# Two cross-attentions in one kernel: where the next context is split, and what the key transfers wait for

## The reference

```
x = x + tanh(g_xattn[0]) * attention_0(layernorm(x), context)     # 16 heads of 32
x = x + tanh(g_ffn[0])   * bit_linear_conv_ffn(layernorm(x))
x = x + tanh(g_xattn[1]) * attention_1(layernorm(x), context, mask)  # 8 heads of 64
x = x + tanh(g_ffn[1])   * fp4_ffn(layernorm(x))

attention: q = x Wq; k = context Wk; v = context Wv
           softmax(q k^T / sqrt(d)) v, heads joined, times Wo
```

## Time and profile before

| | before |
|---|---|
| median of 3 executions | 2663.02 us |
| profiled execution: time | 2659.33 us |
| profiled execution: span, mean granted clock of TensorE | 2657.5 us, 0.885 |
| PE (matmuls) busy | 2027.9 us, 76% |
| DVE busy | 1655.1 us, 62% |
| ACT busy | 952.9 us, 36% |
| POOL busy | 950.8 us, 36% |
| weight loads of PE (beside the matmuls) | 1410.6 us, 53% |

### The profile page before, as it was taken

How to read it: one execution, slowest core, us unless ns; L and a number is a source line. 1 busy time by engine, 2 the same in 40 slices (tenths; PEclk the granted TensorE clock), 3 DMA queues, 4 the chain that set the end, 5 groups by cost and what they waited for, 6 DMA issues and landing times. The chain is left out here.

```text
span 2657.5 us, 42241 instructions
## 1 busy us (share of the span) xinstructions
PE 2027.9 (76%) x15208; PEld 1410.6 (53%) x15208; DVE 1655.1 (62%) x3011; ACT 952.9 (36%) x1299; POOL 950.8 (36%) x518
## 2 busy tenths in 40 slices
PE   3688888788887078888489999998997125788887
PEld 2366566566565077777246666666665113344443
DVE  3656655665662887887444455545543998777773
ACT  2155555555566223333224443444434111111110
POOL 4054444444456321221302222222224563433442
PEclk8898998999896589999689999999998557888888
DMA  4232322333220301010433323333321200001000
GB/s 156 56 82 70 96 78 76 91 88 85 78 57 25 138 15 40 23 41 28 140 84 92 104 79 93 102 102 81 92 79 41 93 30 12 20 28 32 24 20 28
DMA packets 152278, 179.25 MB, mean 67 GB/s; under 512 B 60456, under 2 KB 120104, under 8 KB 151592
## 3 DMA queue, kind: packets, MB, share of 16 engines
q1 hardware_dynamic: 152104, 176.86, 23.1%
HBM read 129.96 MB, written 46.60 MB: 66 GB/s over the span
## 5 line engine op out<-in xcount | busy, mean ns | idle before, releaser
L545 POOL TENSOR_TENSOR a_p_hl<-a_p,a_p_hl 125x1344 bf16<-125x1344 f32 x192 | 525.0, 2735 | 953.9 <-ACT a_p_hl L643 953.3
L871 PE MATMUL a_psum<-a_chl,a_w 128*128 128x375 bf16 x1536 | 305.0, 356 | 55.4 <-DVE a_chl L718 45.6
L960 PE MATMUL a_psum<-a_k_st,a_q_st 96*112 96x375 bf16 (+2 forms) x1024 | 257.2, 344 | 111.3 <-DVE a_nm L778 68.9
L643 ACT ACTIVATE a_p_hl<-a_p 125x1344 bf16<-125x1344 f32 x192 | 254.0, 1323 | 121.7 <-PE a_psum L978 118.8
L633 ACT ACTIVATE a_p<-a_psum 125x1344 f32<-125x1344 f32 x192 | 247.8, 1291 | 132.5 <-PE a_psum L940 128.7
L871 PE MATMUL a_psum<-a_w,a_chl 128*125 128x512 bf16 x1152 | 269.8, 384 | 1.5 <-DVE a_xnT L748 0.9
L778 DVE TENSOR_REDUCE a_nm<-a_psum 112x1 f32<-112x750 f32 x256 | 236.1, 930 | 49.7 <-PE a_psum L960 47.4
L871 PEld LDWEIGHTS a_psum<-a_chl,a_w 128*128 128x128 bf16 x1536 | 158.0, 106 | 176.6 <-issue 88.3
L940 PE MATMUL a_psum<-a_q_st,a_k_st 99*125 99x224 bf16 (+2 forms) x1536 | 222.6, 268 | 5.2 <-ACT a_p L633 5.1
L960 PEld LDWEIGHTS a_psum<-a_k_st,a_q_st 96*112 96x112 bf16 (+2 forms) x1024 | 107.6, 131 | 196.3 <-DVE a_nm L778 89.6
L978 PEld LDWEIGHTS a_psum<-a_v_st,a_p_hl 125*128 125x128 bf16 x4608 | 180.4, 99 | 39.5 <-issue 22.9
(11 more groups left out here) (203 smaller groups left out, 3388.6 us busy)
## 6 DMA issues: line engine op xcount, KB each, us to landing
a_k_st<-a_k SPq DMA_DIRECT2D x192, 187.5 KB, 3.4
a_c<-in_ctx_t SPq DMA_DIRECT2D x32, 750.0 KB, 5.4
a_k<-a_k_tmp SPq DMA_DIRECT2D x64, 375.0 KB, 3.0
a_q_st<-a_q SPq DMA_DIRECT2D x192, 56.0 KB, 2.9
a_q<-a_q_tmp SPq DMA_DIRECT2D x64, 112.0 KB, 1.9
x<-a_xo SPq DMA_DIRECT2D x32, 224.0 KB, 2.3
f_w<-in_w1T SPq DMA_DIRECT2D x4, 1024.0 KB, 11.1
f_w<-in_w2T SPq DMA_DIRECT2D x4, 1024.0 KB, 16.7
```

Source lines behind the costliest of these rows:

```text
L545: nc.gpsimd.tensor_tensor(p_hl[0:MC, h % 2, 1, :], p32[0:MC, h % 2, :], p_hl[0:MC, h % 2, 0, :], ALU.subtract).then_inc(plo_done, 1)
L643: nc.scalar.activation(p_hl[0:MC, par, 0, :], p32[0:MC, par, :], ACT.Copy).then_inc(phi_done, 1)
L871: ins = nc.tensor.matmul(out, lhs, rhs, start=(c == 0 and n == 0), stop=(c == KC - 1 and n == 2))
L960: ins = nc.tensor.matmul(sm_[0:HALF, kh, 0:MK], q_stack(b.parity, at(h), rows)[:, s * HALF:(s + 1) * HALF], k_stack(b.parity, at(h), rows) ...
```

## The change

For items 2 to 7 the first half of the next context is now split in the third quarter, right behind unit K(3, 1) of the item before. SP orders the second half behind the query transfers of chunk 3, still in the third quarter. ACT writes its high part at the start of the fourth quarter, DVE its low part at the second head of the fourth quarter, before that head's units. For item 1, in the prologue, all stays as it was.

On SP one function, `regroup`, replaces two. It serves keys and queries in turn: store, wait for that store alone, then the three transfers into the stack. `kq_sent` becomes `k_sent` and `q_sent`, so an attention has one semaphore more. The semaphores of A0 stay taken until POOL clears and frees them at the start of the first FFN; those of A1 stay taken.

The diff, less the lines that only drop the counter `n_sent`; the condition `b.number == 1` replaces `b.number != 0` on ACT as it does on DVE:

```diff
--- before.py
+++ after.py
@@ -173,8 +173,12 @@
         def pb(name, shape):
             return ctx.enter_context(nc.psum_tensor(f"{tag}_{name}", shape, F32))

+        sems = []
+
         def sem(name):
-            return ctx.enter_context(nc.semaphore(f"{tag}_{name}"))
+
+            sems.append(nc.alloc_semaphore(f"{tag}_{name}"))
+            return sems[-1]


         q_dram = nc.dram_tensor(f"{tag}_q", (KC, 2, P, S), BF16, kind="Internal").ap()
@@ -240,7 +244,7 @@
         st_in = [sem(f"st_in{c}") for c in range(KC)]
         m_in = [sem(f"m_in{g}") for g in range(2)]
         out_sent = sem("out_sent")
-        kq_sent = sem("kq_sent")
+        k_sent, q_sent = sem("k_sent"), sem("q_sent")
         sp_steps = sem("sp_steps")
         preset = sem("preset")
         w_hi, w_lo, gate_ready = sem("w_hi"), sem("w_lo"), sem("gate_ready")
@@ -393,31 +396,22 @@
                 sp.dma_start(x_out[bass.ds(at, 1), s:s + 1, :, :].rearrange(
                     "o s p d -> p (o s d)"), xo[:, s, :]).then_inc(out_sent, 16)

-            def send_k(cc, n_done):
-
+            def regroup(b, cc, n_done, sent, tmp, dram, stack, width, parts):

                 sp.wait_ge(unit_done, n_done)
-                sp.dma_start(k_dram[cc].rearrange("a p m -> p a m"), k_tmp[:, cc % 2, :, :]).then_inc(kq_sent, 16)
-
-            def send_q_and_regroup(b, cc, n_done):
-
-                n_done, n_both = value(n_done), value(n_sent.next() * 32)
+                sp.dma_start(dram[cc].rearrange("a p n -> p a n"), tmp[:, cc % 2, :, :]).then_inc(sent, 16)
                 n_used = value((b.index - 1) * H + (cc + 1) * HC)
-                sp.wait_ge(unit_done, n_done)
-                sp.dma_start(q_dram[cc].rearrange("a p s -> p a s"), q_tmp[:, cc % 2, :, :]).then_inc(kq_sent, 16)
-
-                sp.wait_ge(kq_sent, n_both)
+                n_sent = value((b.index * KC + cc + 1) * 16)
                 if b.number is None or b.number >= 2:
                     settle()

                     sp.wait_ge(st_ready, n_used)
-                for stack, tmp, width, parts in ((k_st, k_dram, M, (0, 1, 0)), (q_st, q_dram, S, (0, 0, 1))):
-                    for (row, col), part in zip(((0, 0), (32, 0), (64, 0)) if stacked else ((0, 0), (64, 0), (0, 8)),
-                                                parts):
-                        c0 = col + cc * HC
-                        sp.dma_start(stack[row:row + DK, b.parity, c0 * width:(c0 + HC) * width].rearrange(
-                            "p (h n) -> p h n", h=HC), tmp[cc, part].rearrange(
-                            "(h p) n -> p h n", h=HC)).then_inc(st_in[cc], 16)
+                sp.wait_ge(sent, n_sent)
+                for (row, col), part in zip(((0, 0), (32, 0), (64, 0)) if stacked else ((0, 0), (64, 0), (0, 8)), parts):
+                    c0 = col + cc * HC
+                    sp.dma_start(stack[row:row + DK, b.parity, c0 * width:(c0 + HC) * width].rearrange(
+                        "p (h n) -> p h n", h=HC), dram[cc, part].rearrange(
+                        "(h p) n -> p h n", h=HC)).then_inc(st_in[cc], 16)

             def move_maxima(b, g, n_done):
                 sp.wait_ge(unit_done, n_done)
@@ -431,9 +425,9 @@
                 kind, k, b = unit
                 n = units.next()
                 if kind == "K" and k[1] == 1:
-                    send_k(k[0], value(n))
+                    regroup(b, k[0], value(n), k_sent, k_tmp, k_dram, k_st, M, (0, 1, 0))
                 elif kind == "Q":
-                    send_q_and_regroup(b, k, n)
+                    regroup(b, k, value(n), q_sent, q_tmp, q_dram, q_st, S, (0, 0, 1))
                 elif kind == "M":
                     move_maxima(b, k, n)
                 elif kind == "OP":
@@ -456,13 +450,12 @@
                     load_x(b + 2)
                     load_ctx(b + 2, 0)
                     load_masks(b + 2)
-                if q == 3:
-                    if (b + 2).exists():
-                        load_ctx(b + 2, 1)
                 if q == 0 and (b + -1).exists():
                     load_residual(b + -1)
                 for unit in quarter_units(q, b) + last_unit(q, b):
                     after_unit(unit)
+                    if unit[:2] == ("Q", KC - 1) and (b + 2).exists():
+                        load_ctx(b + 2, 1)


             sp.sem_inc(out_sent, 1)
@@ -659,22 +650,28 @@

             def quarter(q, b):
                 if q == 3 and (b + 2).exists():
-                    split_ctx(b + 2, 0, units.base + units.k)
+                    split_ctx(b + 2, 1, units.base + units.k)
                 if q == 1 and (b + 1).exists():
                     mask_bias_t(b + 1)
                 slots = slots_of(q, b)
+
+                def unit_step(unit):
+                    unit_hi_part(unit)
+                    if unit[:2] == ("K", (KC - 1, 1)) and (b + 2).exists():
+                        split_ctx(b + 2, 0, None)
+
                 for j in range(HC):
                     for unit in slots[4 * j]:
-                        unit_hi_part(unit)
+                        unit_step(unit)
                     if b.exists():
                         exponentials(b, q * HC + j)
                     for unit in slots[4 * j + 1]:
-                        unit_hi_part(unit)
+                        unit_step(unit)
                     if b.exists():
                         exponentials_hi(b, q * HC + j)
                     for k in (2, 3):
                         for unit in slots[4 * j + k]:
-                            unit_hi_part(unit)
+                            unit_step(unit)
                 if q == 3 and (b + 2).exists():
                     mask_bias(b + 2)
                 for unit in last_unit(q, b):
@@ -720,7 +717,7 @@

             def unit_lo_part(unit):
                 kind, k, b = unit
-                if unit[:2] == ("K", (0, 0)) and b.number != 0:
+                if unit[:2] == ("K", (0, 0)) and b.number == 1:
                     split_ctx(b, 1)
                 n = units.next()
                 bank = units.bank()
@@ -809,14 +806,20 @@
                     unit_lo_part(step)

             def quarter(q, b):
-                if q == 3 and (b + 2).exists():
-                    split_ctx(b + 2, 0)
                 slots = slots_of(q, b)
+
+                def unit_step(unit):
+                    unit_lo_part(unit)
+                    if unit[:2] == ("K", (KC - 1, 1)) and (b + 2).exists():
+                        split_ctx(b + 2, 0)
+
                 for j in range(HC):
                     h = q * HC + j
+                    if q == 3 and j == 1 and (b + 2).exists():
+                        split_ctx(b + 2, 1)
                     for k in (0, 1):
                         for unit in slots[4 * j + k]:
-                            unit_lo_part(unit)
+                            unit_step(unit)
                     preparing = q == 2 and (b + 2).exists()
                     if preparing and j == HC - 1:
                         normalise(b + 2)
@@ -1019,13 +1022,15 @@

             walk(pe.Fori, quarter, prologue, units.enter_loop, units.leave_loop)

+    return sems
+

 LINKS_PER_ROW = 44 - 14

 ROUND = 1.5 * 2.0 ** 23


-def bit_ffn(nc, tag, x_in, x_out, w1T, conv_w, conv_b, w2T, gate):
+def bit_ffn(nc, tag, x_in, x_out, w1T, conv_w, conv_b, w2T, gate, old_sems):

@@ -1185,6 +1190,7 @@

         @block.gpsimd
         def _(pool):
+            nc.clear_and_free_semaphores(old_sems)
             nc.gpsimd.memset(ones[:, :], 1.0).then_inc(preset, 1)
             pool.wait_ge(preset, 1)
             nc.gpsimd.memset(ident[:, :], 0.0).then_inc(preset, 1)
@@ -2018,8 +2024,8 @@
             Wq1, Wkv1, Wo1, w_gate, w_up, w_down, out):

     x1, x2, x3 = (nc.dram_tensor(f"x{n}", (B, 2, HALF, D), F32, kind="Internal").ap() for n in (1, 2, 3))
-    cross_attention(nc, "a0", x, x1, ctx_t, (Wq0T, Wk0T, Wv0T, Wo0T), g_xattn[0:1], None, 16)
-    bit_ffn(nc, "f0", x1, x2, w1T, conv_w, conv_b, w2T, g_ffn[0:1])
+    a0_sems = cross_attention(nc, "a0", x, x1, ctx_t, (Wq0T, Wk0T, Wv0T, Wo0T), g_xattn[0:1], None, 16)
+    bit_ffn(nc, "f0", x1, x2, w1T, conv_w, conv_b, w2T, g_ffn[0:1], a0_sems)
     cross_attention(nc, "a1", x2, x3, ctx_t, (Wq1, Wkv1[:, 0:D], Wkv1[:, D:2 * D], Wo1), g_xattn[1:2],
                     (mask, mask_t), 8)
     fp4_ffn(nc, "f1", x3, out, w_gate, w_up, w_down, g_ffn[1:2])
```

More of the change, by code:

```diff
@@ L334, in _ @@
             units = Units()
-            n_sent = Units(KC)
             def value(v):
@@ L479, in enter @@
                 units.enter_loop(i)
-                n_sent.enter_loop(i)
             def leave():
                 units.leave_loop()
-                n_sent.leave_loop()
             walk(sp.Fori, quarter, prologue, enter, leave)
```

## The result

The change made the kernel slower: 2688.88 us (median of 4 runs, 2685.82 to 2695.31) against 2664.22 us before (4 runs beside them), a ratio of 1.0095 with a 95% interval of 1.0074 to 1.0115. I had forecast 2646 us and a range of 2627 to 2665. The profiled execution took 2688.89 us (span 2687.1, granted clock 0.875 against 0.885), 29.6 us more than the one before.

The account below looks back on a forecast made before the run. PE was taken to set a row's pace, with its waits at the seam between rows to win. A0's rows -15.9, A1's -5.9 and prologues +5.2 made -16.6 us: about 2646 us, range 2627 to 2665.

Parts of the forecast that it names:

- A0's seam: First attention, fourth quarter: the stretch through the second key projection falls from 18.55 to 13.6 us, 4.9 us gained per seam.
- A0's third quarter: First attention: the moved first-half split makes PE wait, 2.0 us per row, plus 0.85 us for a possible clock drop.
- rival C: A0's third-quarter split runs 3.0 us because of POOL's subtraction and the clock falls: slower, 2675 us; chance 0.11.
- A0's transfers: First attention, seam: key stacks go earlier and query stacks at 615.4 instead of 616.1, 0.6 us gained per row.
- A1's seam load: Second attention: the second half's load, behind the third quarter's transfers, lands slightly late for ACT; +0.2 us per row net.
- Rival D: The second half's load takes 7.2 us, ACT stands at both attentions' seams, 21.6 us back: 2668 us; chance 0.17.
- A1's stack waits: Second attention, seams: query stacks go 2 us earlier, so PE's wait for them, 7.1 us over six seams, goes.
- The wait for the split in A1: Second attention, seam: PE's 2.84 us wait before the second key projection, and the slow projection behind it, stay.
- The prologues: Both attentions' prologues: query stores behind the keys' landing lengthen PE's and ACT's waits, 5.2 us together (0 to 8).
- Semaphores: Start of the first FFN: POOL clearing A0's 40 semaphores costs nothing, at most 2 us.

Follow-up runs that it names:

- e1: The kernel before with only the transfers changed (keys: store, wait, stacks; then queries), splits and context loads as before: ratio 0.9992 to the kernel before.
- e4: The changed kernel with the load of the next context's second half issued ahead of the third quarter's query unit, in both attentions: ratio 0.9954 to the kernel before.
- e7: Kernel of e6, with A1's second-half load ahead of the query unit and DVE's split ahead of K(0,0)'s low part: 2612.73 us, 0.9814 to the kernel before.
- e5: Kernel before with splits moved in A0 alone; in both attentions both stores issued first, then keys' and queries' stacks each behind their own store: 2623 us, ratio 0.9855.
- e10: The changed kernel with both stores issued before the keys' stacks for items 0 and 1 only: 2672.06 us, ratio 1.0024 to the kernel before.
- e9: The kernel before with only its transfers changed to the order of e5, splits and loads as before: 2641 us, ratio 0.9905.
- e6: The kernel of e5 with the splits moved in A1 too, the second-half load behind the third quarter's query unit: ratio 0.9834 to the kernel before.

## Why the prediction was wrong

By its own steps:

- **A0's seam (13.6 us, -4.9)**: right, 13.35 us and -5.2.
- **A0's third quarter (+2.0, clock +0.85)**: right. PE waits 2.15 us where it waited 0.35, and the query projection behind takes 1.93 us instead of 1.31, the clock's part. All six splits there take 1.73 us, so rival C did not happen.
- **A0's transfers (-0.6 a row)**: not borne out. The query stacks go 3.5 us behind their store (612.29 to 615.80), where the sum had 2.0 from the earlier trace rows, and the wait for the stacks did not fall: 19.6 us over A0's loop (19.2 in e1), before 18.8. That the row as a whole came out right (-2.7 for -2.65) owes something to luck: this term was too good and the third quarter's too bad (2.2 us from the product at 575.80 to the one at 592.95 against those at 573.97 and 588.96, where the sum had 2.85).
- **A1's seam load (+0.2 a row)**: the step that failed most. Its place and its path, ACT in order and from it PE, were named rightly, and the slack of ACT was 0.7 us (a wait of 4.66 us there reached PE as 3.96) where the sum had 0.8. But ACT waits 2.25 to 4.66 us, and the sum had 1.1. What failed is the chain of landings ahead of the load: the queries' store was priced at a landing of 2.0 us, read in the old order, and takes 2.9 to 3.2 in the new one; the keys' store was priced at 2.9 us and takes 4.6 to 5.0 in three of the six seams (why, no run shows). So the load was issued 10.15 to 12.55 us behind the keys' store and not 8.9. The load's own length, 4.8 us, was right in five of six seams; the 7.6 us of the earlier trace rows is the load of the first half, issued at 1699.9, and the six loads of the second half took 4.6 to 4.8 us before the change. Rival D, at 0.17, had the place of the loss but not its reason: it rested on a load of 7.2 us. It also saw ACT wait in A0, where the load was in time. And the cost of being late was mis-sized: D gave it 2.5 us a row and set it against rows that gain; measured are 4.3 us net of a stack wait that went, 5.6 us by e4. The clock was left out there: behind the wait for the maximum both key projections run at the lower level, and e4 gives back about as much by the clock (17 us) as by the waits (22 us).
- **A1's stack waits (-7.1)**: right, 7.1 to 0.9 us, and worth more than that (e1: 12.8 us over six rows).
- **The wait for the split in A1 (2.8 us, unchanged)**: right, and e7 shows that it was not bound to stay.
- **The prologues (+5.2, bounds 0 to 8)**: wrong, +22.0 by the marks, 16.0 of it up to PE's wait for the last chunk. I priced the two waits of PE and ACT in the earlier trace rows and let each grow by one step. The queue of SP's issues in the prologue, which I did not read, shows that SP has no free time there: it is the engine that sets the pace, and each chunk pays the second landing, 2.0 us in A0. With the order of e5 a chunk of A0's prologue takes 5.95 us (e5), 6.3 (e10) or 6.8 (e9), before 6.97, and e10 shows that this order alone takes the loss away.
- **Semaphores (0)**: no loss; the first FFN was 2.1 us shorter. What of that is the clearing was not tried.

The prologues alone took back as much as the whole sum had promised (16.6 us), and A1's rows, at +26.0 instead of -5.9, made the kernel slower.

## What to carry to other kernels

Where one engine issues a chain of store, wait, fetch for several items, add up its time per item and compare it with what the producer needs: where it has no slack, every wait that is put into it counts for each item (here 2.0 us a chunk), and here it was better to issue both stores first and then wait for them in order. A load that is moved behind other waits on an in-order queue has to be priced from its issue: here the load's own length held and the landings ahead of it, read in the old order, did not. Set that issue against the slack of the in-order engine that wants the load first; 2.3 to 4.7 us too late there cost 5.6 us a row, by way of the next engine and its clock.

## What the runs showed of the hardware

The same store of 112 KB of queries lands in 1.9 us (median of 64) when it is issued before the key stacks' transfers, and in 3.2 us when it is issued right behind them, on the same queue. The fetches of the query stacks behind it get shorter in exchange, 2.9 to 2.2 us:

```profile
a_q_st<-a_q SPq DMA_DIRECT2D x192, 56.0 KB, 2.2
a_q<-a_q_tmp SPq DMA_DIRECT2D x64, 112.0 KB, 3.2
```

In e5, e6 and e9, with the stores first, it is 1.8 to 1.9 us again. A landing time read in one order of the queue did not hold in another: the change's order itself made the number wrong that its forecast used.
